# A gated cross-attention kernel: the first attention reads x as loaded, and its norm is applied to the result

## The reference

```python
def _layernorm(x, axis=-1, eps=1e-05):
    m = jnp.mean(x, axis=axis, keepdims=True)
    v = jnp.var(x, axis=axis, keepdims=True)
    return (x - m) / jnp.sqrt(v + eps)

# first attention: queries and keys come from ctx alone
query = jnp.einsum('bnc,dc->bnd', teacher_features, Wq) + bq
key = jnp.einsum('bnc,dc->bnd', teacher_features, Wk) + bk
energy = jnp.einsum('bnd,bmd->bnm', query, key)
attention = jax.nn.softmax(energy, axis=-1)
x_m = jnp.einsum('bln,bmn->blm', teacher_logits, attention)

x = x + jnp.tanh(g_xattn[0]) * L0_xattn(layernorm(x), ctx, ...)
x = x + jnp.tanh(g_ffn[0])   * L0_ffn(layernorm(x), ...)     # quantised 704-wide layer
x = x + jnp.tanh(g_xattn[1]) * L1_xattn(layernorm(x), ctx, ...)  # 16 heads
x = x + jnp.tanh(g_ffn[1])   * L1_ffn(layernorm(x), ...)     # 64 experts, top 8
```

## Time and profile before

| what | value |
|---|---|
| median of 3 runs | 615.57 us (615.5 to 616.37) |
| span of the profiled execution | 614.4 us |
| PE busy / DVE busy / ACT busy / POOL busy | 604.4 / 477.4 / 422.5 / 235.1 us |
| granted TensorE clock | 1.00 throughout |

### The profile page before, as it was taken

The page is one execution under the profiler, slowest core; times in us unless marked ns, Lnnn a source line. Parts: engine busy times, 40 slices in busy tenths (PEclk is TensorE's granted clock), DMA queues, the critical chain, the costliest instruction groups (busy, mean ns, idle before and its releaser), DMA issues.

```text
span 614.4 us, 11617 instructions
## 1 busy us (share of the span) xinstructions
PE 604.4 (98%) x3644; PEld 525.1 (85%) x3644; DVE 477.4 (78%) x1139; ACT 422.5 (69%) x1082; POOL 235.1 (38%) x280
## 2 busy tenths in 40 slices
PE   8989999999999999999999999999999999999997
PEld 6757899999999999999998888888887888887886
DVE  3999988887777787688876787788777676777776
ACT  6999999888888888889897344465444444443442
POOL 5899998576665566656662020000000000000000
PEclk9999999999999999999999999999999999999999
DMA  8513302000000000000030544353856466555640
GB/s 294 201 53 102 92 13 78 2 2 2 2 1 2 1 2 2 1 2 1 11 121 2 169 150 152 128 171 97 215 156 167 116 174 175 153 158 152 188 133 34
DMA packets 33653, 56.47 MB, mean 92 GB/s; under 512 B 12800, under 2 KB 13504, under 8 KB 33600
## 3 DMA queue, kind: packets, MB, share of 16 engines
q1 hardware_dynamic: 33312, 55.82, 30.5%
q10 hardware_dynamic: 288, 0.00, 0.0%
HBM read 53.45 MB, written 1.31 MB: 89 GB/s over the span
## 4 chain that ended last, share of the span: by engine, by line
PE 87%; DVE 5%; ACT 3%; POOL 2%; issue 2%; DVEq 0%; POOLq 0%; ACTq 0%
PE bank L299 25%; PE bank L301 24%; PE bank L300 24%; PE bank L968 4%; PE bank L943 2%; PE bank L935 2%; DVE hs L2072 1%; PE bank L895 1%; PE bank L1009 1%; PE bank L815 1%; PE bank L821 1%; PE bank L888 1%; ACT w L1461 1%; PE bank L801 1%; POOL att L585 1%
## 5 line engine op out<-in xcount | busy, mean ns | idle before, releaser
L1607 ACT ACTIVATE inter_hi<-inter 128x512 fp32r<-128x512 f32 x63 | 39.8, 632 | 140.6 <-DVE inter L2271 140.6
L299 PE MATMUL bank<-xnT_hi,front_hi 128*128 128x512 f32 (+1 forms) x260 | 102.0, 392 | 0.0
L301 PE MATMUL bank<-xnT_hi,front_lo 128*128 128x512 f32 (+1 forms) x260 | 101.7, 391 | 0.0
L300 PE MATMUL bank<-xnT_lo,front_hi 128*128 128x512 f32 (+1 forms) x260 | 101.7, 391 | 0.0
L2275 DVE TENSOR_TENSOR inter_lo<-inter,inter_hi 128x512 fp32r<-128x512 f32 x63 | 43.6, 692 | 37.9 <-ACT inter_hi L1607 37.3
L1559 ACT ACTIVATE att<-bank,shift,rq 128x256 f32<-128x256 f32 x128 | 71.2, 572 | 0.0
L585 POOL TENSOR_TENSOR att<-att,rowinv 128x512 f32<-128x512 f32 x60 | 63.1, 1067 | 11.7 <-DVE rowinv L2171 11.7
L2244 DVE TENSOR_TENSOR prod<-gate_s,bank 128x512 f32<-128x512 f32 x63 | 43.2, 686 | 21.7 <-PE bank L301 19.6
L2154 DVE TENSOR_REDUCE rowmax<-bank 128x2 f32<-128x512 f32 x64 | 43.6, 685 | 21.0 <-PE bank L301 20.7
L300 PEld LDWEIGHTS bank<-xnT_lo,front_hi 128*128 128x128 f32 x260 | 48.9, 188 | 11.3
L301 PEld LDWEIGHTS bank<-xnT_hi,front_lo 128*128 128x128 f32 x260 | 48.8, 188 | 11.3
(11 more groups left out here) (271 smaller groups left out, 1813.1 us busy)
## 6 DMA issues: line engine op xcount, KB each, us to landing
w_all<-w_rows SPq DMA_DIRECT2D x128, 128.0 KB, 3.0
raw<-in_expert_w SPq DMA_DIRECT2D x32, 384.0 KB, 3.5
wvo_raw<-in_expert_w SPq DMA_DIRECT2D x16, 384.0 KB, 3.6
e_more<-in_expert_w SPq DMA_DIRECT2D x16, 384.0 KB, 3.6
raw<-in_head_qk SPq DMA_DIRECT2D x8, 384.0 KB, 3.2
wvo_raw<-in_head_vo SPq DMA_DIRECT2D x4, 384.0 KB, 3.8
w_keep<-in_head_vo SPq DMA_DIRECT2D x4, 384.0 KB, 3.6
gate_raw<-in_gate_wT SPq DMA_DIRECT2D x2, 704.0 KB, 8.8
```

The lines of the kernel that those rows point to most:

```text
L299: pe.matmul(out, l_hi, r_hi_, start=start, stop=False, skip_group_check=True)
L300: pe.matmul(out, l_hi, r_lo_, start=False, stop=False, skip_group_check=True)
L301: return pe.matmul(out, l_lo, r_hi_, start=False, stop=stop, skip_group_check=True)
L1607: act.activation(inter_hi[:, slot, :], inter[:, slot, :], ACT.Copy).then_inc(a_Ihi, 1)
```

## The change

TensorE turns `x` itself as it came from memory, and waits only for its load. GpSimd no longer writes `u` for this attention; instead it makes two small values for every row: `tg_rstd`, the inverse root times tanh(g), and `tg_mean`, the mean times `tg_rstd`. `add_A` multiplies the product by `tg_rstd`, one instruction for each tile, since a scalar of each row belongs to one tile. The constant `tg_mean` of a row is taken off later, in `add_output`, again one instruction for each tile. The calls of `turn_rows_0(0)`, `turn_rows_0(1)` and `copy_rows_0(0)` stand earlier.

```diff
             def root_0(b):
                 c = slice(2 * b, 2 * b + 2)
                 pool.wait_ge(v_pw1, b + 1)
-                pool.tensor_scalar(negm[:, c], mv[:, c, 0], -1.0, 0.0, ALU.mult, ALU.add)
                 pool.tensor_scalar(vare[:, c], mv[:, c, 1], 1.0, EPS, ALU.mult, ALU.add).then_inc(g_va0, 1)
...
-                pool.tensor_tensor(rstd[:, c], vare[:, c], minus_half[:, 0:2], ALU.pow).then_inc(g_pw1, 1)
+                link_g(pool, pool.tensor_tensor(rstd[:, c], vare[:, c], minus_half[:, 0:2], ALU.pow))
+                if b == 0:
+                    pool.wait_ge(a_tg, 1)
+                link_g(pool, pool.tensor_scalar(tg_rstd[:, c], rstd[:, c], tg[:, 0:1], 0.0, ALU.mult, ALU.add))
+                pool.tensor_tensor(tg_mean[:, c], mv[:, c, 0], tg_rstd[:, c], ALU.mult).then_inc(g_pw1, 1)
...
-            def normalise_0(i):
-
-                pool.wait_ge(g_pw1, i // 2 + 1)
-                pool.tensor_scalar(u[:, i, :], x[:, i, :], negm[:, i:i + 1], rstd[:, i:i + 1], ALU.add,
-                                   ALU.mult).then_inc(g_u0, 1)
...
             def turn_rows_0(b, bk):
-                pe.wait_ge(g_u0, 2 * b + 2)
+                pe.wait_ge(l_x[b // 2], 16)
...
-                                          u[:, 2 * b + t, k * P:(k + 1) * P], ident[:, :])
+                                          x[:, 2 * b + t, k * P:(k + 1) * P], ident[:, :])
...
             energy(0, 2)
+            turn_rows_0(0, 1)
             query_key(1, 2, 0)
             energy(1, 6)
             energy(2, 0)
-            turn_rows_0(0, 1)
             pe.wait_ge(a_eA, 4)
             turn_att(0, 6)
             energy(3, 3)
             mix(0, 1)
+            turn_rows_0(1, 5)
             turn_att(1, 2)
-            turn_rows_0(1, 5)
...
             copy_qk(0, 2, 4, 3)
+            copy_rows_0(0, 1)
             copy_qk(1, 2, 5, 0)
             exp_A(0, 2)
             exp_A(1, 6)
-            copy_rows_0(0, 1)
...
             def add_A(b, bk):
                 dve.wait_ge(t_oA, b + 1)
-                if b == 0:
-                    dve.wait_ge(a_tg, 1)
-                xb = x[:, 2 * b:2 * b + 2, :]
-                dve.scalar_tensor_tensor(xb, bank4(bk), tg[:, 0:1], xb, ALU.mult, ALU.add).then_inc(v_xA, 1)
+                dve.wait_ge(g_pw1, b + 1)
+                for t in range(2):
+                    i = 2 * b + t
+                    ins = dve.scalar_tensor_tensor(x[:, i, :], bank4(bk)[:, t, :], tg_rstd[:, i:i + 1], x[:, i, :],
+                                                   ALU.mult, ALU.add)
+                ins.then_inc(v_xA, 1)
...
             def add_output(b):
                 dve.wait_ge(t_Y, 16 * b + 16)
-                xb = x[:, 2 * b:2 * b + 2, :]
-                dve.tensor_tensor(xb, bank4(YBK), xb, ALU.add).then_inc(v_Y, 1)
+                for t in range(2):
+                    i = 2 * b + t
+                    ins = dve.scalar_tensor_tensor(x[:, i, :], bank4(YBK)[:, t, :], tg_mean[:, i:i + 1], x[:, i, :],
+                                                   ALU.subtract, ALU.add)
+                ins.then_inc(v_Y, 1)
```

More of the change, by code:

```diff
@@ L75, in flamingo_kernel @@
         rstd = sb("rstd", [P, TILES])
+        tg_rstd = sb("tg_rstd", [P, TILES])
+        tg_mean = sb("tg_mean", [P, TILES])
         u = sb("u", [P, TILES, HID])
@@ L159, in flamingo_kernel @@
         g_gain, v_sc1, v_sc2, g_sc1, g_sc2 = (sem(n) for n in ("g_gain", "v_sc1", "v_sc2", "g_sc1", "g_sc2"))
-        g_u0, t_u0, a_x0 = sem("g_u0"), sem("t_u0"), sem("a_x0")
+        t_u0, a_x0 = sem("t_u0"), sem("a_x0")
         g_u1, v_u, t_u, a_u, c_u = sem("g_u1"), sem("v_u"), sem("t_u"), sem("a_u"), sem("c_u")
@@ L602, in _ @@
             power_0(0)
-            normalise_0(0)
-            normalise_0(1)
             root_0(1)
             power_0(1)
-            normalise_0(2)
-            normalise_0(3)
             root_0(2)
             power_0(2)
-            normalise_0(4)
-            normalise_0(5)
             scale_gain(g1, l_g1)
@@ L623, in _ @@
             limit_1(0)
-            normalise_0(6)
             scale_back_1(1)
             scale_gain(g2, l_g2)
-            normalise_0(7)
             limit_1(1)
```

## The result

| kernel | median of 6 runs | span of the profiled execution |
|---|---|---|
| before, run beside it | 615.65 us (615.48 to 616.37) | 614.4 us |
| changed | 617.62 us (617.56 to 619.03) | 615.9 us |

The ratio is 1.0038, with an interval of 1.0028 to 1.0048; the medians differ by 1.97 us. The kernel became slower by about twice the 1.03 us of the forecast sum. In every run whose span is on record the time is 1.74 to 1.88 us above the span: the changed kernel's 615.9 us belongs to a run of 617.67. By the same distance the 614.4 us of before stand for an execution of about 616.2 us (an estimate), 0.6 above its median.

The account below looks back on a forecast made before the run. TensorE's own work bounds the kernel after 60 us, so only earlier lateness counts: 0.79 us from transposes and copy plus 0.24 from add_A splits, 1.03 us in all, giving 616.6 us; range 615.2 to 618.0.

Parts of the forecast that it names:

- What bounds it: After 60 us TensorE's own work; only lateness made before TensorE is saturated, or a long later wait, changes the time.
- rival 1: Slack at the handovers at 28.44 us and before 54.88 us absorbs the lateness: 615.6 us; chance 0.14.
- The first and second four transposes: On TensorE, each four delay what follows by 0.44 us; ScalarE hands over to VectorE 0.79 us late.
- Splits of `add_A`: On VectorE, each split costs 0.12 us; the two in its stretch, add_A(2) and add_A(3), give 0.24 us.
- The later additions: The four split add_output on VectorE, up to 1.0 us more in all, hidden behind full TensorE: 0.
- GpSimd's relief: GpSimd has 4.6 us less to do, worth 0 because its lead is lost in waiting; otherwise 0.69 us gain.
- Rival 2: GpSimd was the hidden bound; less contention with VectorE's low_w and 0.69 us gain 1.28 us: 614.3 us; chance 0.09.
- Rival 3: GpSimd's long calls meet other VectorE instructions, adding 0.59 us, upper ends 0.46: 2.1 us slower, 617.6; chance 0.27.
- the sign: In the trace, another two-input VectorE instruction grown longer would show contention with GpSimd falling worse.
- The range: Overall time of 615.2 to 618.0 us.
- the forecast's own range: Half a microsecond either side of 616.6 us: 616.1 to 617.1 us; the forecast's chance 0.50.
- The sign "near 55.9": If right, TensorE's transposes of the second layer's rows start near 55.9 us, with no gaps behind.

Follow-up runs that it names:

- e1: The changed kernel with turn_rows_0(0), turn_rows_0(1) and copy_rows_0(0) called at their old places; 617.17 us, ratio 1.0024.
- e4: The kernel before with each add_A split into two 128x256 instructions, nothing else; 615.57 us, ratio 1.0003.
- e8: The changed kernel with add_output as one plain 128x512 addition, the subtraction of tg_mean left out; 617.56 us, ratio 1.0033.
- e11: The changed kernel with four extra GpSimd instructions of 128x2, results unread, ahead of limit_1(1); 618.37 us, ratio 1.0038.
- e3: The changed kernel with round_1(3) called before add_A(2) on VectorE, nothing else; 617.03 us, ratio 1.0024.

## Why the prediction was right and wrong

- **What bounds it**: right. TensorE is full behind 60 us in both, and all that was made ahead arrives, so rival 1 is out. The 1.17 us between span and median were the 1.8 between a run's time and its span, less the 0.6 by which the profiled execution lay above the median; the forecast of the time does not hang on it.
- **The first and second four transposes**: right, 0.44 and 0.79 us; e1 took exactly 0.79 off again. Taking the start-to-start 0.44 and not the 0.60 was right.
- **Splits of `add_A`**: each is 0.13 for 0.12, but the second stands ahead of an instruction held by GpSimd, which ends when GpSimd ends; its lateness goes up in the hold (after, e4). The term is 0.13, not 0.24. That the earlier trace rows have `add_A(3)` in their chain does not make its growth arrive.
- **The later additions**: right, nothing (e8).
- **GpSimd's relief**: this is the step that failed. I took 0, "so a lead is lost in waiting", with 0.69 us of gain as the only other end. The lead is lost in waiting, 1.91 us of it, but not before it has done harm: 0.69 us less on GpSimd put `times_gain` ahead of `round_1(3)`, and that cost 0.92 us. The step counted GpSimd only as a supplier and not as an opponent. Its 4.6 us of relief were 3.8.
- **Rival 2**: did not come; `low_w(1)` still took 1.54 us, at 35.80.
- **Rival 3** named this mechanism and put 0.59 us on one meeting, the excess at 34.66. It was one meeting, of another VectorE instruction with a `times_gain`, and 0.92; not one of two inputs, as the sign had it, but a rounding of one tensor by a scalar of each row. The 0.59 was no property of the pair: a hold lasts from the start of the loser to the end of the winner, less some 0.2 us, here up to 1.50 us. Its other 0.46 us, from splits and transposes at their upper ends, did not come. That the measured 617.62 falls on its 617.6 is luck in the size.
- **The range** held the time only because it took in that rival; the forecast's own range, 616.1 to 617.1, did not. The sign "near 55.9" came out by luck: the transposes start at 56.01, but only because after's profiled execution started 0.70 us earlier. By S they are 1.83 late and not 1.03.
- **Not foreseen**: the fall back of 0.2 us behind 130 us.

The Trainium skill (SBUF — State Buffer, Who interferes with whom) says that VectorE and GpSimd share one pair of ports to SBUF, and that against a VectorE instruction in a two-port mode it is held for a whole instruction by whoever issues first, while the other blocks fully; it counts `tensor_scalar` among those that can enter such a mode, and lets an instruction with two SBUF inputs contend as well. This case's traces agree for `round_1(3)`: ends at 31.71 behind 31.56, 31.35 behind 31.20, and in e11, where both start at 30.50, 32.34 behind 32.20. In which mode it ran no trace says. That rule should have been laid on the order in the earlier trace rows: `round_1(3)` at 30.23, and a `times_gain` behind the 0.69 us that the change removes.

## What to carry to other kernels

When a change takes work off GpSimd, list the element-wise VectorE instructions on SBUF within a GpSimd instruction's length of each moved GpSimd instruction, and see for each pair who starts first before and who will after; the price is from the loser's start to the winner's end, less some 0.2 us here (31.56 - 30.45 = 1.11 for the 0.92 measured, 1.70 for the 1.50 of e11). Where nothing waits for the relieved engine, try another place in its list, or call the victim ahead (e3): here either took off more than the relief gave, which was nothing. And take the lateness from a common point behind the start, not from the span, before a difference of 1 us is explained.

## What the runs showed of the hardware that was not expected

- A hold can absorb lateness as well as make it: `sc` took 0.40, 0.26 and 0.27 us (before, after, e4) and what stood behind it kept its place relative to GpSimd.
- A near tie goes with 0.43 us more or less. GpSimd's power and VectorE's rounding near 51 us start within 0.01 to 0.02 us of each other in all 14 profiled executions, the rounding first; the power took 0.71 us in ten of them and 1.12 in four, 0.02 us apart (51.54 and 51.56) in e1 and 0.02 us apart in before too, where it took 0.71. That the tie decides is not shown, and H doesn't tell why the power, starting second, keeps its length in ten. Part of the spread of some 1 us between runs of one kernel may come from it and part from the start; neither was tried.
- Not all of VectorE is held. Beside `times_gain` at 29.59 to 31.32 (e3) the additions with their product in PSUM and the statistics kept their lengths of 0.86 for two and 0.75.
- The first products of queries and keys on TensorE run at about half pace (in before they start some 0.43 us apart, and 0.22 from 7.14 us on) for a stretch that ends between 5.5 and 7.1 us, depending on the execution, while the profile shows a granted clock of 1.00 (before, 5.30 to 7.10 us); it moves the start of everything by up to 1 us. The cause is open.
